# Expert layer of a small perceiver: rows gathered by a token table, and expert products in three rounded parts

## The reference, cut to what matters

```
xn   = layernorm(x);  y0 = rmsnorm(xn)                 # 2048 x 256, y = y0 * rms_w
pick = top 2 of 8 experts of (y @ gate_w.T), softmax over the two
for each token and each of its two experts e:
    h   = silu(y @ W1[e].T) * (y @ W2[e].T)            # 256 -> 704, twice
    out += prob * (h @ W3[e].T)                        # 704 -> 256
x = x + xn + out                                       # residual
```

## Time and profile before

| | us |
|---|---|
| median of 3 runs | 3599.68 (3596.82 to 3601.22) |
| profiled execution | 3602.53, span 3600.7 |
| granted TensorE clock, mean | 0.954 |

### The profile page before, as it was taken

One profiled execution on the slowest core, in us unless ns is written; L12 is line 12 of the kernel. 1 busy time (PEld: TensorE's weight loads), 2 busy tenths in 40 slices (PEclk: granted clock), 3 DMA queues, 4 the chain that ended last, 5 costly groups with the idle time before them and its releaser, 6 DMA issues. The chain is left out here.

```text
span 3600.7 us, 131563 instructions
## 1 busy us (share of the span) xinstructions
PE 3272.5 (91%) x56310; PEld 2646.8 (74%) x56311; DVE 2493.8 (69%) x4543; ACT 2188.4 (61%) x3459; POOL 1490.2 (41%) x1443
## 2 busy tenths in 40 slices
PE   9999999999888399979999999999885888888889
PEld 6888888888777266647888888888634666666667
DVE  5777777777644122237767777777659999999976
ACT  5666666666553022226666666666667888888843
POOL 4433333333122300035333333333007899999930
PEclk8999999999987699979999999999998999999989
DMA  2000000010003410111100000000001111111110
GB/s 81 31 31 31 31 31 31 31 33 29 12 2 142 173 32 29 32 67 47 40 31 31 31 31 31 31 31 22 28 9 39 45 45 49 49 48 47 48 35 24
DMA packets 61320, 147.86 MB, mean 41 GB/s; under 512 B 8962, under 2 KB 29186, under 8 KB 60514
## 3 DMA queue, kind: packets, MB, share of 16 engines
q1 hardware_dynamic: 57154, 130.26, 11.2%
q0 software_dynamic: 3072, 8.39, 0.7%
q10 hardware_dynamic: 544, 1.05, 0.1%
HBM read 122.89 MB, written 16.78 MB: 39 GB/s over the span
## 5 line engine op out<-in xcount | busy, mean ns | idle before, releaser
L805 ACT ACTIVATE x_probs<-x_score_ps 128x1024 f32<-128x1024 f32 (+1 forms) x896 | 814.6, 961 | 616.8 <-PE x_score_ps L631 585.4
L910 DVE TENSOR_REDUCE x_maxes<-x_misc_ps 128x1 f32<-128x512 f32 (+1 forms) x1792 | 1022.8, 627 | 37.0 <-PE x_misc_ps L549 31.5
L842 POOL CAST x_kT_hi<-x_kT 128x512 fp32r<-128x512 f32 (+1 forms) x448 | 254.3, 568 | 1141.5 <-ACT x_kT L708 1112.4
L2566 DVE TENSOR_TENSOR_SCAN b_state<-b_decay_ps,b_drive 128x512 f32<-128x512 f32 x512 | 598.0, 1210 | 17.0 <-POOL b_drive L2505 10.4
L625 PE MATMUL x_score_ps<-x_qz,x_kT 32*128 32x128 f32 x13312 | 593.4, 277 | 1.5 <-issue 1.0
L625 PEld LDWEIGHTS x_score_ps<-x_qz,x_kT 32*128 32x128 f32 x13312 | 502.9, 182 | 6.8 <-issue 4.6
L596 PE MATMUL x_misc_ps<-x_probs,x_v 128*32 128x64 f32 x26624 | 465.2, 221 | 0.5 <-issue 0.2
L596 PEld LDWEIGHTS x_misc_ps<-x_probs,x_v 128*32 128x32 f32 x26624 | 392.7, 110 | 77.9 <-issue 24.5
L549 PE MATMUL x_misc_ps<-x_kT_hi,x_qz_hi 32*128 32x512 f32 (+1 forms) x2048 | 430.6, 406 | 5.6 <-DVE x_u L977 1.4
L2327 PE MATMUL b_turn_ps<-ident,b_state 128*128 128x128 f32 x2048 | 293.0, 285 | 141.8 <-DVE b_state L2566 71.3
L2505 POOL TENSOR_TENSOR b_drive<-b_b_all,b_xc 128x1024 f32<-128x1024 f32 x160 | 376.7, 2376 | 28.4 <-DVE b_state L2566 28.2
(11 more groups left out here) (326 smaller groups left out, 5961.0 us busy)
## 6 DMA issues: line engine op xcount, KB each, us to landing
x_raw<-in_ctxT SPq DMA_DIRECT2D x64, 800.5 KB, 4.5
b_b_all<-b_b_rows SPq DMA_DIRECT2D x128, 256.0 KB, 3.3
m_w<-in_m_w SPq DMA_DIRECT2D x16, 704.0 KB
m_w<-in_m_w SPq DMA_DIRECT2D x8, 768.0 KB
m_slot_rows<-m_zero SPq DMA_DIRECT2D x1, 4992.0 KB, 17.4
m_block_rows<-m_slot_rows SPq DMA_DIRECT2D x39, 128.0 KB, 2.0
m_slot_out<-m_out SPq DMA_DIRECT2D x39, 128.0 KB, 1.7
x<-in_x SPq DMA_DIRECT2D x4, 512.0 KB, 6.4
```

The lines of the kernel that those rows point to most:

```text
L805: nc.scalar.activation(probs[rows, s % 2, js, 0:n], score_ps[rows, js, 0:n], ACT.Exp).then_inc(exp_done, 1)
L910: nc.vector.tensor_reduce(maxes[:, c:c + m, j, k0 // NB], bank(op)[:, 0:m * even].rearrange("p (c k) -> p c k", c=m)[:, :, 0:kn], AX.X, AL ...
L2566: nc.vector.tensor_tensor_scan(order(state[:, k % 2, c, :]), order(decay_ps[:, c % 2, :]), order(drive[:, h % 3, c % 2, :]), 0.0, ALU.mult ...
```

## The change: what it does

Instead of scattering every token's row to two slots, the kernel writes the normalised rows once, in token order, to DRAM (`normed_rows`, two plain transfers on POOL's queue), and finds for each slot the token that it holds: `in_block` has, for a token and a block, the token's number if its slot is in that block; `at_place` is 1 where the slot's place within the block is the column; 32 matmuls sum their products to a table of 128 places by 39 blocks. Unused slots get token 0. POOL then gathers each block's 128 rows with one indirect DMA: blocks 0 and 1 at the end of `route`, block b when PE has transposed block b-2. The residual on `x_sb` moves from the end of DVE's stream to just behind the normalised rows. The zero fill and its memset go. `at_place` lies in the memory of `xnT`. ACT runs one Silu activation at the end of `route`.

The products with W1 and W2 become three fp32r matmuls each. The weights are split anew for every block, in four quarters (W1 and W2, two halves of the 704 columns each) of 2x352 values per partition, held once: ACT rounds a quarter when PE has used the one before it (`w_used`), DVE makes the rest.

```diff
 route:
-        sp.wait_ge(zeroed, 1)
-        sp.dma_start(slot_rows..., zero... broadcast).then_inc(zero_out, 16)
 pe:
+        for i in range(2):
+            for t in range(NT):
+                if t % PART == 0:                       # PART = NT // 2
+                    pe.wait_ge(placed, i * 2 + t // PART + 1)
+                ins = nc.tensor.matmul(gate_ps[:, 0:SLOT_BLOCKS], at_place[:, i, t, :], in_block[:, i, t, :],
+                                       start=i == 0 and t == 0, stop=i == 1 and t == NT - 1)
+        ins.then_inc(tokens_found, 1)
 dve:
+        (behind rows) wait rows_done; 16 x tensor_scalar(x_sb[:, t, :], ...)       # was last
-        nc.vector.tensor_copy(slot[:, :, :], slot_f[:, :, :]).then_inc(slot_done, 1)
+        link: slot_block = slot_f / P - (P - 1) / (2P);  + ROUND;  - ROUND        # 3 tensor_scalar, [P, 32]
+        link: slot_within = slot_block * -P + slot_f
+        for i in range(2):
+            link(in_block[:, i] = (slot_block[:, i] == blocks))                     # [P, 16 x 39]
+            in_block[:, i] *= tokens                                                # [P, 16 x 39]
+            for t in range(0, NT, PART):
+                at_place[:, i, t:t + PART] = (slot_within == within)  .then_inc(placed, 1)   # [P, 8 x 128]
+        nc.vector.tensor_copy(slot[:, :, :], slot_f[:, :, :])
         link(ended ...)
+        dve.wait_ge(tokens_found, 1)
+        nc.vector.tensor_copy(slot_token[:, :], gate_ps[:, 0:SLOT_BLOCKS]).then_inc(tokens_done, 1)
 pool:
-        32 x indirect scatter; pool.wait_ge(scattered, 16 * 2 * NT)
+        for t in range(0, NT, PART):
+            pool.wait_ge(rows_done, t + PART)
+            nc.gpsimd.dma_start(normed_rows...[:, t:t + PART, :], rows[:, t:t + PART, :]).then_inc(rows_out, 16)
+        pool.wait_ge(rows_out, 32)
+        pool.wait_ge(tokens_done, 1)
+        for b in range(2):
+            fetch_block(nc, normed_rows, slot_token, block_rows, b).then_inc(rows_in[b], 16)
 expert_blocks, pool:
+        for b in range(2, SLOT_BLOCKS):
+            pool.wait_ge(rows_turned, b - 1)
+            fetch_block(nc, normed_rows, slot_token, rows, b).then_inc(rows_in[b % 2], 16)
 sp:  -  the loads of rows
 pe, products:                                             # value_load of the expert goes
-            8 matmuls, yT x w[expert], float32
+            for g in range(4):
+                pe.wait_ge(w_lo_done, n * 4 + g + 1)
+                for k in range(KD):
+                    for m, (y, w) in enumerate(((y_hi, w_hi), (y_hi, w_lo), (y_lo, w_hi))):
+                        matmul(dst[:, g % 2, 0:HN], y[:, j, k, :], w[:, g, k, :], ...)
+                ins.then_inc(w_used, 1)
 act, step n:                                              # round_quarters: value_load, then a Copy for each quarter
         hT copy
+            round_quarters(n + 2, range(3), True)         # each waits for w_used of block n + 1
         silu(n + 1);  take_rows(n + 2)                    # take_rows now writes y_hi, two Copies
+            round_quarters(n + 2, range(3, 4), True)
 dve, step n:
         two hT copies
+            rest_of_quarters(n + 2, range(3))             # value_load; each waits for w_hi_done, subtracts [P, 704]
         hidden(n + 1)
+            keep_rest(n + 2, j)                           # y_lo, two scalar_tensor_tensor [P, 128]
+            rest_of_quarters(n + 2, range(3, 4))
         out copy
 act, start:  take_rows(0); wait w_in; 4 quarters of block 0; take_rows(1); quarters 0 to 2 of block 1; silu(0); quarter 3
```

More of the change, by code:

```diff
@@ L34 @@
 M_CONST_PARTS = [("rows_before", P), ("ones", P), ("experts", NE), ("tile_chain", NE * NT), ("whole_blocks", NT),
-                 ("blocks", SLOT_BLOCKS)]
+                 ("blocks", SLOT_BLOCKS), ("within", P), ("tokens", NT)]
 M_CONST = sum(n for _, n in M_CONST_PARTS)
@@ L1509, in route @@
     prefix_done = sem("m_prefix_done")
-    slot_done = sem("m_slot_done")
+    placed = sem("m_placed")
+    tokens_found = sem("m_tokens_found")
+    tokens_done = sem("m_tokens_done")
     seq = sem("m_seq")
@@ L1589, in _ @@
         nc.scalar.activation(expo[:, :], gap[:, :], ACT.Exp).then_inc(e_done, 1)
+        nc.scalar.activation(silu_warm[:, :], root[:, 0:1], ACT.Silu)
     @block.vector
@@ L1636, in _ @@
                                     ALU.subtract, ALU.mult).then_inc(rows_done, 1)
+        dve.wait_ge(rows_done, NT)
+        for t in range(NT):
+            nc.vector.tensor_scalar(x_sb[:, t, :], x_sb[:, t, :], gain[:, t:t + 1], offset[:, t:t + 1], ALU.mult, ALU.add)
         dve.wait_ge(c_in, 32)
@@ L1712, in expert_blocks @@
     out_ps = ps("m_out_ps", [P, NB])
-    rows_in = [sem(f"m_rows_in{j}") for j in range(2)]
     rows_turned = sem("m_rows_turned")
+    y_hi_done = sem("m_y_hi_done")
     yT_done = sem("m_yT_done")
-    up_done = sem("m_up_done")
+    w_hi_done = sem("m_w_hi_done")
+    w_lo_done = sem("m_w_lo_done")
+    w_used = sem("m_w_used")
     gate_done = sem("m_gate_done")
@@ L1738, in steps, with expert, quarter @@
             step(b // 2, b % 2, b)
+    def expert(engine, n):
+        return engine.value_load(block_expert[0:1, ds(n, 1)], min_val=0, max_val=NE - 1)
+    def quarter(g, e):
+        return (w1, w2)[g // 2][:, ds(e, 1), :, g % 2 * HN:(g % 2 + 1) * HN].rearrange("p e k n -> p (e k) n")
     def exists(b, ahead):
@@ L1757, in step @@
                          out[:, j, :]).then_inc(stored[j], 16)
-        for j in range(2):
-            load(0, j)
         steps(sp, step)
@@ L1825, in take_rows, with round_quarters @@
             for c in range(KD):
-                ins = nc.scalar.activation(yT[:, j, c, :], yT_ps[:, c * P:(c + 1) * P], ACT.Copy, scale=rms_w[:, c:c + 1])
-            ins.then_inc(yT_done, 1)
+                ins = nc.scalar.activation(y_hi[:, j, c, :], yT_ps[:, c * P:(c + 1) * P], ACT.Copy, scale=rms_w[:, c:c + 1])
+            ins.then_inc(y_hi_done, 1)
+        def round_quarters(n, of, free):
+            e = expert(act, n)
+            for g in of:
+                if free:
+                    act.wait_ge(w_used, n * 4 - 4 + g + 1)
+                nc.scalar.activation(w_hi[:, g, :, :], quarter(g, e), ACT.Copy).then_inc(w_hi_done, 1)
         def silu(n):
-            act.wait_ge(up_done, n + 1)
+            act.wait_ge(w_used, n * 4 + 4)
             act.wait_ge(h_done, n)
@@ L1851, in _, with keep_rest, rest_of_quarters @@
     def _(dve):
+        def keep_rest(n, j):
+            dve.wait_ge(y_hi_done, n + 1)
+            for c in range(KD):
+                ins = nc.vector.scalar_tensor_tensor(y_lo[:, j, c, :], yT_ps[:, c * P:(c + 1) * P], rms_w[:, c:c + 1],
+                                                     y_hi[:, j, c, :].bitcast(F32), ALU.mult, ALU.subtract)
+            ins.then_inc(yT_done, 1)
+        def rest_of_quarters(n, of):
+            e = expert(dve, n)
+            for g in of:
+                dve.wait_ge(w_hi_done, n * 4 + g + 1)
+                nc.vector.tensor_tensor(w_lo[:, g, :, :], quarter(g, e), w_hi[:, g, :, :].bitcast(F32), ALU.subtract
+                                        ).then_inc(w_lo_done, 1)
         def hidden(n):
@@ L1868, in step, with _ @@
             nc.vector.tensor_copy(out[:, j, :], out_ps[:, 0:D]).then_inc(out_done, 1)
+        keep_rest(0, 0)
+        rest_of_quarters(0, range(4))
+        keep_rest(1, 1)
+        rest_of_quarters(1, range(3))
         hidden(0)
+        rest_of_quarters(1, range(3, 4))
         steps(dve, step)
+    @block.gpsimd
+    def _(pool):
+        for b in range(2, SLOT_BLOCKS):
+            pool.wait_ge(rows_turned, b - 1)
+            fetch_block(nc, normed_rows, slot_token, rows, b).then_inc(rows_in[b % 2], 16)
 def mamba(nc, x_sb, ident, a, index, index_in):
@@ L3032, in program @@
         self_attention(nc, x_sb, ident, a)
-        experts(nc, x_sb, ident, a, prob, slot, slot_out)
+        rows_out = sem("m_rows_out")
+        rows_in = [sem(f"m_rows_in{j}") for j in range(2)]
+        experts(nc, x_sb, ident, a, prob, slot, slot_out, rows_out, rows_in)
         xattn(1, returned=(prob, slot, slot_out))
```

102 lines of the change are left out of this document (57 added, 45 removed).

## The result

| us | before | after |
|---|---|---|
| median (4 runs each) | 3600.41 (3596.82 to 3601.22) | 3544.23 (3540.02 to 3547.33) |
| profiled execution, span | 3602.53, 3600.7 | 3540.02, 3537.2 |
| ratio | | 0.9845, interval 0.9828 to 0.9862 |

Forecast was 3544, range 3533 to 3564. Where the time went is best read from marks inside the layer, since they leave out what varies above it. Marks: DVE starts the operation behind the last slot; PE starts the idle transposes of the second program block ("block" in the table); DVE starts the first h and the last h (39 blocks, 38 steps); DVE starts its last output copy. The last column is the sum.

The account below looks back on a forecast made before the run. PE bounds the expert loop; gate products, DVE's chain, POOL's scatters and block end bound routing. 3602.5 - 23.7 (routing) + 0.7 (first block) - 32.7 (loop) = 3546.8, less 2.85 from profiled execution to median: 3544 us, range 3533 to 3564.

Parts of the forecast that it names:

- table, 64 records: Routing: PE's 64 float32 table records at 0.214 us each take 13.7 us and set the table's end.
- table's end to POOL's last issue done: Routing: DVE's copy of the table, then POOL's issue of two gathers, 2.6 us.
- that to the block's start: Routing's block end: 4.0 us from POOL's last issue to PE's idle transposes, between 2 and 5.8.
- slots to block, gained: Routing: table and gather in place of the scatter let PE's next block start 23.7 us earlier.
- first h later: Way into the loop: splitting the first quarters delays the start by 0.7 us, within 0.4 to 1.0.
- product record, 352 columns: Loop: one fp32r matmul of 352 columns takes 0.161 us, on a line between the 256- and 512-column rows.
- period: Loop: one block takes 7.68 us in place of 8.54, 0.86 less, with PE still last.
- loop, gained: Expert loop: 38 blocks at 0.86 us less each gain 32.7 us.
- spare time of h: Loop: DVE finishes h 1.2 us before PE needs it for the h transposes.
- The rival of a full clock: Routing rival, 9%: PE runs the table at 2.4 GHz, 0.107 us a record, ending 6.8 us sooner; 3537 us.
- DVE as the bound: Loop rival, 14%: DVE's list reaches 8.2 us a block and sets the period, 19 us more; 3563 us.
- Cover: Routing: POOL's plain transfers, up to 7.8 us each, and weights ending between 1187 and 1196 are hidden.

Follow-up runs that it names:

- the kernel with transposes ahead: 36 idle transposes of the identity put between count product and table on PE, against the changed kernel; 3541.94 us, ratio 0.9830 to the kernel before.
- the run with one more subtraction: One more DVE subtraction of 704 elements ahead of h in each block, result unused, against the changed kernel; 3544.49 us.
- the kernel with the split only: Three-part products alone, with scatter, zero fill and SP's loads kept, against the kernel before; 3571.83 us, ratio 0.9916.
- the kernel with one part: Only hi x hi of the three product parts made, all splits kept, against the changed kernel; 3479.53 us.

## Why the prediction was right, step by step

| step | forecast us | measured us |
|---|---|---|
| slots to first table record | 3.7 | 3.72 |
| table, 64 records | 13.7 (0.214 each) | 13.87 |
| table's end to POOL's last issue done | 2.6 | 3.50 |
| that to the block's start | 4.0 | 3.67 |
| slots to block, gained | 23.7 | 22.92 |
| first h later | 0.7 | 0.09 |
| product record, 352 columns | 0.161 | 0.16 |
| period | 7.68 | 7.64 |
| loop, gained | 32.7 | 34.8 |
| spare time of h | 1.2 | 1.0 |
| weights land | 1187 to 1196 | about 1181 |

*Table.* The nearest row (8 columns behind the same loads, at the same clock) had the price of 39 columns, 0.214 beside 0.217 a record. So between 8 and 39 columns the columns don't matter; that it is the weight load that sets the price is the reading that fits, for the loads fill 13.73 of the 13.87 us. The rival of a full clock failed by the clock row (0.50 with 13.87 of 13.95 busy), and in the kernel with transposes ahead even a clock given beforehand was lost.

*The way to the gather.* The term that was too small, by 0.9 us. DVE's copy starts at 1185.33 and POOL's first gather at 1186.38, 0.85 after the copy's end, where the forecast had none. The shorter block end gave 0.3 of it back.

*First block.* PE's first product came 3.28 us after its first row transposes, 1.0 more than before, as forecast (0.4 to 1.0). It was repaid by products 0.94 shorter (first product to silu, 4.09 in place of 5.03), a gain that the forecast had counted for 38 blocks and not for the first, and by 0.2 from shorter idle transposes (4.21 us in place of 4.40). Another 0.2 was lost between silu and h, while DVE finished rests. The 0.2 of the transposes is luck: they took up to 4.79 in kernels with the same code up to there.

*Loop.* The line between the 256- and the 512-column row held. The 2.1 us more than forecast have two sources. A block became 0.91 shorter on average (8.547 to 7.638), not 0.86: 38 x 0.048 = 1.8 us. The products gave 0.82 of it (4.73 to 3.91), and 0.08 came from the time between h's transposes and the next product, which fell from 0.71 to 0.63. And in the kernel before the first step took 8.81 us, 0.3 more than the others, in the kernel after it did not. The last step is 0.23 shorter than the rest in both kernels (8.32 and 7.41), which cancels.

*DVE as the bound.* It did not happen, and the run with one more subtraction says how near it was: some 0.24 us of spare time was left. The forecast of 1.2 was 0.2 too large. DVE still stood 1.5 us a block for ACT's first rounding (55.8 us in 37 waits). The collision that it leaned on did not come from the gathers' issues: none of the 156 rests takes over 0.893 us, with 39 gathers beside them. It came when GpSimd was given casts and subtractions of its own. The kernel before had shown it already: the 1.09 us that the rival cites the earlier trace rows is the time of a subtraction of the feed-forward layer at 3482.10 (L2974) that ran beside a GpSimd cast (L2914, 3481.57 to 3482.64); from 3500 to 3592, where GpSimd is idle, the same subtractions take 0.68 to 0.69 us.

*Cover.* The plain transfers of the rows took POOL 1.29 and 0.94 us (bound: 7.8 each) and 14.0 us to landing (median of two), so they were in by about 1158, 28 us before the first gather. The DMA share is 0.52 in 1180 to 1182 and 0.00 behind, so the weights ended at about 1181; with the layer's start 5.7 later, as in the kernel before, that is the lower end of the forecast.

The sum by the profiled executions was 3602.5 - 55.7; it measured 3540.0, 6.8 lower, of which 5.7 are the earlier start of the layer. The median's exact hit (3544.23 for 3544) is luck: the terms of this layer are off by -0.8 in routing, +0.6 at the first block and +2.1 in the loop, 1.9 us in all, and the time of the rest of the kernel moves by several us from one execution to the next. That each term came out within 2.1 us, by the wait and the engine that the forecast named, is not luck.

## What to carry to other kernels

Matmuls of 8 to 40 columns behind the same weight load had the same price here at the same clock, so for few columns look for a row with the same load and clock, and halve the records before trying to raise the clock. Work moved to a helper engine is free up to that engine's spare time, and adding one operation, then two, measures the spare time better than a sum of durations does; take the time by which the next operation starts later, not the durations. When GpSimd gets real work on SBUF, place it where VectorE waits. Two halves of a change, run alone, can each be worth less than their share: here the gather's gain in the loop shows only with the short products.

## What the runs showed that was not expected

- A rounded (fp32r) record of 40 columns costs as much as a float32 record at clock 0.50, about 0.22 against 0.214 us; its gain is that there is one in place of two.
- The clock fell from 1.00 to 0.50 with PE busy without a gap, within a run of float32 matmuls of 39 columns that had begun after 1.5 us of idleness.
- VectorE's subtractions took 1.58 us each (6.33 / 4) in place of 0.82 (3.30 / 4) beside two GpSimd casts and a subtraction.
- A wait for rows that PE didn't feel by itself held back a register load behind it, and with it the W3 product, by 0.25 us in every second step of the kernel with the split only (a reading of the trace, not tested).
- The same gate products ran at 0.96 us for 8 records in one execution and 1.71 in another, with nothing edited there (the slots were known 35.0 us after the start of the stage at the earliest, in the kernel with one part, and 39.3 at the latest, in the kernel before).
